# Row loads of the source stage: one DMA per pair of tiles into eight slots

## What is computed

```python
# second layer: x is (6250, 128), edge_attr (206250, 64), row/col the ends of each edge
h = jnp.maximum(_layernorm(x, axis=-1), 0.0)
msg = jnp.concatenate([h[row], h[col], edge_attr], axis=-1)
hid = jax.nn.relu(msg @ W1 + b1)           # 256 wide
msg_out = hid @ W2 + b2
x = x + jax.ops.segment_sum(msg_out, row, num_segments=6250)
```

## Time and profile before

| | |
|---|---|
| median of 3 runs | 5701.07 us |
| the profiled execution | 5682.86 us |
| its span, from the first to the last instruction | 5681.1 us |
| TensorE busy (matmul) | 5111.3 us, 90% |
| VectorE busy | 3923.1 us, 69% |
| ScalarE busy | 2971.1 us, 52% |
| POOL busy | 3871.0 us, 68% |
| moved by DMA | 995.58 MB, mean 175 GB/s |

### The profile page before, as it was taken

How to read it: one execution, slowest core, us unless ns; L and a number is a source line. 1 busy time by engine, 2 the same in 40 slices (tenths; PEclk the granted TensorE clock), 3 DMA queues, 4 the chain that set the end, 5 groups by cost and what they waited for, 6 DMA issues and landing times.

```text
span 5681.1 us, 160364 instructions
## 1 busy us (share of the span) xinstructions
PE 5111.3 (90%) x34188; PEld 4074.0 (72%) x34189; DVE 3923.1 (69%) x14222; ACT 2971.1 (52%) x8485; POOL 3871.0 (68%) x3713
## 2 busy tenths in 40 slices
PE   4888888888888886999999999999997999999999
PEld 3777777777777774677666666666665888887788
DVE  6777877878778776555455555555455888888887
ACT  3566666666666653333333333332223777777776
POOL 4777777777777774677777777777776555555553
PEclk7889889889889987999999999999998999999999
DMA  4522222222222234999888988888886999999997
GB/s 109 165 54 54 54 54 54 54 54 54 54 54 54 54 105 139 278 275 270 262 263 258 266 262 260 262 264 259 262 257 186 224 221 222 222 221 217 217 222 193
DMA packets 860128, 995.58 MB, mean 175 GB/s; under 512 B 307993, under 2 KB 663225, under 8 KB 859776
## 3 DMA queue, kind: packets, MB, share of 16 engines
q1 hardware_dynamic: 662496, 610.19, 39.9%
q0 software_dynamic: 190592, 379.87, 24.6%
q10 hardware_dynamic: 6816, 3.38, 0.2%
HBM read 728.41 MB, written 264.62 MB: 175 GB/s over the span
## 4 chain that ended last, share of the span: by engine, by line
PE 59%; DMA 9%; issue 9%; DVE 9%; POOL 8%; DVEq 3%; ACT 3%; POOLq 0%; ACTq 0%; SPq 0%
PE bank L1703 12%; PE bank L1536 12%; PE bank L1626 8%; PE bank L1628 7%; PE bank L1693 7%; DMA xr<-arena 6%; POOL xr L547 5%; PE bank L1457 3%; POOL arena L499 2%; DVE arena L945 2%; DVEq L251 2%; DVE arena L1048 2%; PE bank L1616 1%; DMA arena<-xr 1%; DVE arena L1028 1%
## 5 line engine op out<-in xcount | busy, mean ns | idle before, releaser
L499 POOL DMA_INDIRECT arena<-h_tab,arena x1612 | 1557.1, 966 | 543.0 <-issue 420.7
L547 POOL DMA_INDIRECT xr<-arena x1612 | 1568.5, 973 | 511.7 <-issue 352.6
L1536 PE MATMUL bank<-arena 128*128 128x136 f32 x6448 | 1311.0, 332 | 78.3 <-DVE arena L1048 11.0
L719 ACT ACTIVATE arena<-bank 128x256 f32<-128x256 f32 x1612 | 591.3, 384 | 1389.6 <-PE bank L1628 932.0
L1626 PE MATMUL bank<-arena 128*128 128x256 f32 x3224 | 1023.4, 400 | 91.8 <-DVE arena L1244 45.1
L1536 PEld LDWEIGHTS bank<-arena 128*128 128x128 f32 x6448 | 980.9, 214 | 162.6 <-DVE arena L1048 67.0
L561 POOL DMA_INDIRECT arena<-p_tab,arena x428 | 671.3, 1569 | 622.3 <-DMA arena<-p_tab,arena 498.4
L626 ACT ACTIVATE arena<-bank 128x256 bf16<-128x256 bf16 x1612 | 614.7, 381 | 792.8 <-PE bank L1457 708.6
L1628 PE MATMUL bank<-arena 128*128 128x256 f32 x3224 | 971.3, 383 | 0.0
L1703 PE MATMUL bank<-arena 128*128 128x257 f32 x3424 | 901.5, 386 | 6.3 <-issue 2.6
L1048 DVE TENSOR_TENSOR arena<-arena,bank 128x272 f32 x1612 | 693.6, 430 | 212.7 <-PE bank L1536 186.0
(11 more groups left out here) (260 smaller groups left out, 6595.3 us busy)
## 6 DMA issues: line engine op xcount, KB each, us to landing
arena<-xr SPq DMA_DIRECT2D x428, 520.0 KB
arena<-q_tab SPq DMA_DIRECT2D x1612, 128.0 KB
arena<-in_edge_attr SPq DMA_DIRECT2D x61, 832.0 KB
arena<-rel_tab SPq DMA_DIRECT2D x124, 224.0 KB
arena<-h_tab,arena POOLq DMA_INDIRECT x1612
xr<-arena POOLq DMA_INDIRECT x1612
arena<-rel_tab SPq DMA_DIRECT2D x124, 192.0 KB
xr<-arena SPq DMA_DIRECT2D x26, 520.0 KB
```

Of the source, the lines that this page charges most:

```text
L499: pool.indirect_dma_start(G[:, q, t, :], None, h_tab, bass.IndirectOffsetOnAxis(ap=idx[:, q, t:t + 1], axis=0)).then_inc(sem(f"gath{q}"), 16)
L547: pool.indirect_dma_start(xr, bass.IndirectOffsetOnAxis(ap=pos[:, q, t:t + 1], axis=0), Rb[:, t, :], None).then_inc(sem(f"scat{m}"), 16)
L1536: last = pe.matmul(PSB[3 + t % 2][:, k * H * MW:(k + 1) * H * MW], OH[:, (t + 2 * q) % 4, k * P:(k + 1) * P], flat(msg[:, t, :, :]), start ...
```

## The change

Each load takes one pair (260 KB), and there are eight slots of one pair; the memory is the same. A load waits for the relu of the pair eight before it. The hot rows of each pair wait for that pair's own load, and the index of an odd pair is made with its own hot rows. Which pairs are gathered stays as it is, and so does the number of gathers, and each gather still waits for the gather two before it. The eight slots' semaphores `slot_in0` to `slot_in7` are shared with the loads of `x` at the kernel's start, hence the offsets in LOADED.

```diff
-CP = 2
-NS = 4
+CP = 1
+NS = 8
 SB = CP * NS
...
-        added = lambda s, k: k == 1
-        NADD = [[k for k in range(CP) if added(s, k)] for s in range(NS)]
+        added = lambda s, k: s % 2 == 1
+        LOADED = [2, 2, 2, 2, 2, 2, 4, 1]
...
-                sp.dma_start(xs[:, c * NC:(c + 1) * NC, :], rows(x, c)).then_inc(sem(f"x_in{c}"), 16)
+                sp.dma_start(xs[:, c * NC:(c + 1) * NC, :], rows(x, c)).then_inc(sem(f"slot_in{c}"), 16)
...
                 if not first:
                     sp.wait_ge(sem("hid_ready"), c * CP - (NS - 1) * CP)
-                sp.dma_start(XR[:, s, :, :], xr[bass.ds(c * (CP * GR), CP * GR), :].rearrange("(k p j) w -> p k (j w)", p=P, j=PR)).then_inc(sem(f"xr_in{s}"), 16)
+                sp.dma_start(XR[:, s, :, :], xr[bass.ds(c * (CP * GR), CP * GR), :].rearrange("(k p j) w -> p k (j w)", p=P, j=PR)).then_inc(sem(f"slot_in{s}"), 16)
...
             def source_add(i, s):
 
-                n = NS // 2 * i + s // 2
-                pool.wait_ge(sem("idx_ready"), NB + NS * i + s + 1)
-                pool.wait_ge(sem(f"gath{s % 2}"), GSUM + 16 * len(NADD[s]) * n)
+                pool.wait_ge(sem("idx_ready"), NB + NS // 2 * i + s // 2 + 1)
+                pool.wait_ge(sem(f"gath{s // 2 % 2}"), GSUM + 16 * (NS // 4 * i + s // 4))
                 pool.nop(nofuse=True)
-                for k in NADD[s]:
-                    pool.indirect_dma_start(XR[:, s, k, RW:RW + HID], None, p_tab,
-                                            bass.IndirectOffsetOnAxis(ap=sidx[:, s, k:k + 1], axis=0),
-                                            compute_op=ALU.add).then_inc(sem(f"gath{s % 2}"), 16)
+                pool.indirect_dma_start(XR[:, s, 0, RW:RW + HID], None, p_tab,
+                                        bass.IndirectOffsetOnAxis(ap=sidx[:, s, 0:1], axis=0),
+                                        compute_op=ALU.add).then_inc(sem(f"gath{s // 2 % 2}"), 16)
             pool.wait_ge(sem("p_out"), 16 * NT)
-            for s in range(NS):
+            for s in range(1, NS, 2):
                 source_add(0, s)
             with pool.Fori(1, NTURN) as i:
-                for s in range(NS):
+                for s in range(1, NS, 2):
                     source_add(i, s)
...
                 if added(s, k):
-                    act.wait_ge(sem(f"gath{s % 2}"), GSUM + 16 * len(NADD[s]) * (c + 1))
+                    act.wait_ge(sem(f"gath{s // 2 % 2}"), GSUM + 16 * (c + 1))
...
             def hotp(i, m, first):
                 s, k, g = m // CP, m % CP, SB * i + m
                 if k == 0:
-                    dve.wait_ge(sem(f"xr_in{s}"), 16 * (i + 1))
-                    n = len(NADD[s])
-                    V.tensor_scalar(sidx[:, s, CP - n:], XR[:, s, CP - n:, RW + HID + 1], 0.0, None, ALU.max).then_inc(sem("idx_ready"), 1)
+                    dve.wait_ge(sem(f"slot_in{s}"), 16 * (i + LOADED[s]))
+                    if added(s, k):
+                        V.tensor_scalar(sidx[:, s, :], XR[:, s, :, RW + HID + 1], 0.0, None, ALU.max).then_inc(sem("idx_ready"), 1)
```

More of the change, by code:

```diff
@@ L265, in _ @@
             for c in range(NCH - 1):
-                sp.dma_start(xs[:, c * NC:(c + 1) * NC, :], rows(x, c)).then_inc(sem(f"x_in{c}"), 16)
+                sp.dma_start(xs[:, c * NC:(c + 1) * NC, :], rows(x, c)).then_inc(sem(f"slot_in{c}"), 16)
             r0 = (NCH - 1) * NC * P
-            sp.dma_start(xs[:, NT - NC:NT - 1, :], x[r0:(NT - 1) * P, :].rearrange("(n p) f -> p n f", p=P)).then_inc(sem("x_in6"), 16)
+            sp.dma_start(xs[:, NT - NC:NT - 1, :], x[r0:(NT - 1) * P, :].rearrange("(n p) f -> p n f", p=P)).then_inc(sem("slot_in6"), 16)
             sp.wait_ge(sem("pads"), 2)
-            sp.dma_start(xs[0:96, NT - 1, :], x[(NT - 1) * P:(NT - 1) * P + 96, :]).then_inc(sem("x_in6"), 16)
-            sp.dma_start(xs[96:NLAST, NT - 1, :], x[(NT - 1) * P + 96:N, :]).then_inc(sem("x_in6"), 16)
+            sp.dma_start(xs[0:96, NT - 1, :], x[(NT - 1) * P:(NT - 1) * P + 96, :]).then_inc(sem("slot_in6"), 16)
+            sp.dma_start(xs[96:NLAST, NT - 1, :], x[(NT - 1) * P + 96:N, :]).then_inc(sem("slot_in6"), 16)
             sp.wait_ge(sem("pads"), 1)
@@ L802, in sources @@
                     if not (first and m < 2):
-                        relu(SB * i + m - 2, (m - 2) % SB, NS // 2 * i + (m - 2) // (2 * CP), first)
+                        relu(SB * i + m - 2, (m - 2) % SB, NS // 4 * i + (m - 2) // 4, first)
             sources(0, True)
@@ L806, in _ @@
                 sources(i)
-            relu(NPAIR - 2, SB - 2, NS // 2 * NTURN - 1, False)
-            relu(NPAIR - 1, SB - 1, NS // 2 * NTURN - 1, False)
+            relu(NPAIR - 2, SB - 2, NS // 4 * NTURN - 1, False)
+            relu(NPAIR - 1, SB - 1, NS // 4 * NTURN - 1, False)
             for u, (c, j, n) in enumerate(OUTS):
@@ L835, in centred @@
                 v, m = xs[:, c * NC:(c + 1) * NC, :], mean[:, c * NC:(c + 1) * NC]
-                dve.wait_ge(sem(f"x_in{c}"), 16 + (32 if c == NCH - 1 else 0))
+                dve.wait_ge(sem(f"slot_in{c}"), 16 + (32 if c == NCH - 1 else 0))
                 link(V.tensor_reduce(m, v, AX.X, ALU.add))
```

## The result

The changed kernel takes 5735.81 us (median of 4 runs, 5733.73 to 5738.15); the kernel before took 5700.26 us in the same comparison. The ratio is 1.0063, with a 95% interval of 1.0046 to 1.0081: slower by some 35 us, where 20 us less was forecast, and above the range. The profiled execution took 5733.73 us, its span 5732.0 us, against 5682.86 and 5681.1 before. Of those 51 us between the two profiles some 15 are the luck of before's profiled execution, which lay 17 us under the median of its four runs, while after's lies 2 us under. Differences that are read from these two profiles are too large by that much.

A forecast was written before the change was run, and what follows sets the result against it. Row loads slower than about 4.0 us were taken to stop TensorE in the source stage. Loads -30, index +11, first load -0.5 sum to -20 us: 5681 us forecast, range 5656 to 5732, the forecast's own 5656 to 5690.

The forecast's parts named there:

- Term A: Source stage, row loads: VectorE's waits for them go nearly to nothing, a turn falls from 12.03 to 11.75 us; -30 us.
- the loop of five pairs: From a slot's freeing relu through its load to a later relu: five pairs, 7.22 us available against 6.15 us needed.
- Term B: Source stage, odd pairs' index made one pair later, so POOL's gather starts later and pair 1's relu may wait; +11 us.
- G: Time from a POOL gather's start until it has landed; seen at 5.08 and 4.00 us, taken as 4.55.
- the other odd pairs: Pairs 3, 5 and 7 of a turn, whose gathers lack the loop's pause; nothing was booked for them.
- Rival 2: Late index, gathers behind two small loads: relu waits for them; 5732 us at 5.35 us landing, 5759 at 5.60; chance 0.16.
- Rival 1: No change, 5701 us: load waits go, but pair 1's gather or the loop's pause takes over; chance 0.22.
- Rival 3: DMA engines run full as the loads' beginnings double: share 1.12, +154 us, 5855 us; chance 0.04.
- Waits for loads under 0.3 us a turn: Sign that the forecast is right: VectorE's waits for row loads fall from 1.03 us a turn.
- A turn of 11.8 us: Sign that the forecast is right: eight pairs of the source stage take about 11.8 us, against 12.03 before.
- Two gathers of the same parity less than 5.7 us apart: Sign that the late-index term is right: spacing on POOL where one gather waits for the other.

The follow-up runs named there:

- e5: The changed kernel with odd pairs' index made behind the even pair's hot rows and four gather semaphores instead of two: 5657.2 us, ratio 0.9941.
- e7: The kernel before with four gather semaphores instead of two, nothing else: 5671.6 us, ratio 0.9965.
- e2: The kernel before with only the index of an odd pair moved to its own hot rows, loads unchanged: 5776.8 us, ratio 1.0143.
- e1: The changed kernel with the index of an odd pair made about one pair earlier, behind the even pair's hot rows: 5730.5 us, ratio 1.0055.
- e3: The changed kernel with four gather semaphores instead of two, so four gathers can be in flight: 5714.5 us, ratio 1.0028.
- e6: The changed kernel with each index made at the end of the step before, ahead of the loop's pause, and four gather semaphores: 5698.1 us, ratio 1.0017.
- e8: The changed kernel without row loads after the first turn, so its sums use wrong rows: 5678.5 us (one run).

## Why the prediction was wrong

**Term A, the loads: the mechanism was right, the size shared with another cause.** VectorE's waits for loads went, as the loop of five pairs said; in e5, at the faster pace, 8.0 us are left. With the gathers out of the way a turn takes 11.72 us there, where 11.75 was forecast. That match is in part luck: of the 0.31 us from 12.03 to 11.72 only 0.15 us is between e7 and e5, which differ in the loads (and in the index standing just ahead of or just behind the even pair's hot rows); 0.16 us is between before and e7, where only the gathers' limit changed. The two medians say the same: 5671.6 - 5657.2 = 14 us. So with four gathers in flight the loads are worth about 15 us, not 30. I had read the differences between stretches as the loads' doing alone. With two in flight their worth depends on the index: the change lies 0.80% under e2, where both have it late, and e1 lies 0.55% above the kernel before, where both have it early.

A 260 KB load was put at 3.3 us from slopes. The DMA issues of the changed kernel give 3.9 us as the median from issue to landing, of e5 3.4 us and of e2 (520 KB) 4.5 us:

```profile
arena<-xr SPq DMA_DIRECT2D x856, 260.0 KB, 3.9
```

```profile
arena<-xr SPq DMA_DIRECT2D x856, 260.0 KB, 3.4
```

```profile
arena<-xr SPq DMA_DIRECT2D x428, 520.0 KB, 4.5
```

At the start of the stage the first of the small loads has its reader 2.86 us after its issue, against the 3.79 us of the earlier trace rows:

```profile
4346.66 15.04 SPq L428 DMA_DIRECT2D arena<-xr  x13
4349.52 0.42 DVE L1349 TENSOR_SCALAR arena<-arena 128x128 bf16<-128x128 bf16 x2 [17.95 <-DMA arena<-xr]
```

So a smaller load does land sooner, but how much depends on what is around it.

**Term B, the index: this is where the prediction failed, in two steps.** The first is "I take G in the middle of the two seen, 4.55: smaller loads mean that a gather has less in front of it". The gather does have less in front of it, but other loads then run between its packets, and G stayed nearly where it was: 5.04 us for pair 1 in the timeline above, 5.09 in the median of all against 5.19 before. The working around it was right. With 5.04 us, index and start (1.02 us from 4975.73 to 4976.75) make 6.06 us, which the prediction had at 0.15 + 0.79 + 5.08 = 6.02, and the relu waited 0.62 us where 0.70 was worked out. By the same sum G = 5.04 leaves 0.26 us a turn, +28 us instead of +11. With that alone corrected the forecast would have been no change, not slower. The rule of the Trainium skill that was weighed there (DMA: Bandwidth & Descriptors, Queues, rings and completion order; engines take turns between queues packet by packet) had G unchanged, and the changed kernel agrees in the number. Whether the taking of turns is the reason is not shown: the 317 KB of loads between a gather's packets in the change fit it, the 109 KB before the change, with the first packet at 3.56 us, fit a gather that stands behind a load. In e5 and e7, where gathers start when their index is ready, small loads go with the shorter G (4.91 against 5.38).

**What the term left out.** The second step that failed is that the other odd pairs "lack the pause of the loop and I book nothing for them". Pair 5's relu waits as long as pair 1's (0.87 and 0.78 us in the mean). Its gather is tied to pair 1's by the wait for the gather two before. I had described that wait and not followed it, though the change moves the gather that it holds up. The pause itself is longer too: VectorE stands still for 1.00 us at the turn of the loop (median of the stage), against 0.73 before, and pair 1's index now stands behind it instead of ahead of it. From the change to e5 the turn falls in three steps: by 0.21 us with four in flight (12.45 to 12.24, e3), by 0.13 more with pair 1's index ahead of the pause (12.11, e6), and by 0.39 with all indices ahead of the additions of the step before (11.72, e5). Of these 0.73 us, 0.16 could be won in the kernel before as well (e7).

Put together as an estimate: the loads won 14 us (e7 to e5) and not 30, pair 1's lateness costs 28 us and not 11, and the hold on pair 5's gather, booked at nothing, 20 us (the change to e3). That is +34 us; 35 were measured. The agreement is better than the method: the parts depend on one another, and taken off in another order they have other prices (the index first brings 5 us, e1).

**The rivals.** Rival 2, slower by the late index, had the right place, a relu that waits for its gather. Its price for G = 5.35 was 5732 us, and the measured time is 5735.8, but that nearness is luck. It wanted a longer gather because of two loads in front. In fact pair 1's G did not grow (5.02 us in the median against 5.27 before); its lateness at the old G and the chain from pair 1 to pair 5 did it. Pair 5's own G did grow, from 5.06 to 5.44 us, but in e3, where its gather is not held, it is 4.78. Rival 1 (no change) had G right and its consequence wrong, as it too left out the chain. Rival 3, full DMA engines, is out: their share fell from 0.93 to 0.88. The Trainium skill's advice that was named beside it (DMA: Bandwidth & Descriptors, Bandwidth; batch DMAs to 1 MiB or more) is not borne out for 260 against 520 KB here: e5, with the smaller loads, is 14 us faster than e7, with the same DMA share of 0.94 in both. SP's additional issues cost nothing that shows.

**The signs named beforehand.** Waits for loads under 0.3 us a turn: came true. A turn of 11.8 us: no, 12.45. Two gathers of the same parity less than 5.7 us apart where one waits for the other: no, 5.76 us from 4976.75 to 4982.51. Relu's waits for gathers in every turn were named as the sign of rivals 1 and 2, and came, 233 in some 96 turns.

## What to carry over

When a change starts one transfer earlier and another later, price the later one at the latency it has now; a hope that it will shorten needs a row of its own. Follow every wait on an earlier transfer of the same kind: with two in flight, a late one delays the next but one, and an engine's wait that nobody seems to wait for can still cost time (18 us in e7). An experiment that removes one of two limits in a row can show almost nothing (e1: 5 us), and both together more than all that was lost (e5: 0.0122 in the ratio, 70 us, of which the kernel before could have had 18).

## What the runs showed of the hardware

A gather of 128 rows that adds into SBUF lands 3.75 us after its start with no other loads (e8) and about 5.1 us with row loads under way. With two gathers in flight this is nearly the same whether the loads come as 520 KB or twice 260 KB (5.19 and 5.09 us), though its first packet starts 1.1 us sooner with the small ones; with four in flight it is 5.38 and 4.91 us. With two in flight and the next one starting some 0.7 us behind the landing (4982.51 against 4981.79 above), gathers cannot follow closer than about one in 2.9 us, about the pace of this stage (3.0 us). The row load of 260 KB kept the DMA engines no busier than one of 520 KB: 0.94 at 226 GB/s in e5 and 0.94 at 224 in e7, which has the large ones; 0.88 at 213 to 215 in the change and 0.93 at 221 before.
